# Attention scores in a language-model tower: padded keys against one 32-row matmul per head

## The reference, cut to what matters

```python
q = _bitlinear(x, w_q).reshape(B, T, N_HEADS, D_HEAD)
k = _bitlinear(x, w_k).reshape(B, T, N_HEADS, D_HEAD)
v = _bitlinear(x, w_v).reshape(B, T, N_HEADS, D_HEAD)
attn = jnp.einsum('bqhd,bkhd->bhqk', q, k) * D_HEAD ** (-0.5)
attn = jax.nn.softmax(attn, axis=-1)
out = jnp.einsum('bhqk,bkhd->bqhd', attn, v).reshape(B, T, C)
return _bitlinear(out, w_o)
# around it: h = h + attention(layernorm(h)); then h = h + experts(layernorm(h))
```

## Time and profile before

| | us |
|---|---|
| median of 3 runs | 1735.05 |
| lowest and highest | 1734.72, 1736.13 |
| span of the profiled execution | 1725.5 |
| attention in it, first to last work of the stage | about 276 to 762 |
| a step of the attention in the loop | about 14.7 |
| PE busy over the span | 1609.2 (93%) |
| DVE busy | 1195.8 (69%) |
| ACT busy | 957.5 (55%) |
| POOL busy | 632.1 (37%) |

### The profile page before, as it was taken

One profiled execution on the slowest core, in us unless ns is written; L12 is line 12 of the kernel. 1 busy time (PEld: TensorE's weight loads), 2 busy tenths in 40 slices (PEclk: granted clock), 3 DMA queues, 4 the chain that ended last, 5 costly groups with the idle time before them and its releaser, 6 DMA issues.

```text
span 1725.5 us, 33624 instructions
## 1 busy us (share of the span) xinstructions
PE 1609.2 (93%) x10884; PEld 1354.1 (78%) x10884; DVE 1195.8 (69%) x2292; ACT 957.5 (55%) x1936; POOL 632.1 (37%) x614
## 2 busy tenths in 40 slices
PE   1798886999999999969999999999999999999997
PEld 0444444777777777749999999999999999999996
DVE  2687886999999999866343566666666666655665
ACT  4976774777777777753222355555555555522221
POOL 4655533544444444421750122222222222023343
PEclk9999999999999999989999999999999999999999
DMA  9999981000000000013111366677766777534365
GB/s 311 315 340 341 337 276 53 26 38 37 36 36 36 36 36 31 37 68 115 37 38 49 121 218 232 234 243 251 251 232 234 238 247 247 207 127 139 109 206 196
DMA packets 89868, 274.42 MB, mean 159 GB/s; under 512 B 12640, under 2 KB 13152, under 8 KB 89696
## 3 DMA queue, kind: packets, MB, share of 16 engines
q1 hardware_dynamic: 70688, 223.71, 37.5%
q0 software_dynamic: 17024, 45.97, 8.8%
q10 hardware_dynamic: 2112, 4.19, 0.8%
HBM read 228.14 MB, written 45.69 MB: 159 GB/s over the span
## 4 chain that ended last, share of the span: by engine, by line
PE 54%; DMA 1%; DVE 0%; POOL 0%; ACT 0%; issue 0%; POOLq 0%; DVEq 0%
PE up_ps L1372 12%; PE up_ps L1370 12%; PE up_ps L1371 12%; PE down_ps L1370 6%; PE down_ps L1371 6%; PE down_ps L1372 6%; PE xT_ps L1414 2%; DMA comb<-slot_rows,slot_i 0%; DVE H L1320 0%; DMA xr<-x_turned 0%; DVE xT_lo L1237 0%; POOL comb L1172 0%; ACT xT_hi L1187 0%; DVE H L1312 0%; PE route_ps L1366 0%
## 5 line engine op out<-in xcount | busy, mean ns | idle before, releaser
L1370 PE MATMUL up_ps<-xT_hi,w_hi 128*128 128x256 f32 (+1 forms) x1704 | 483.9, 284 | 8.4 <-DVE xT_lo L1237 8.4
L1372 PE MATMUL up_ps<-xT_hi,w_lo 128*128 128x256 f32 (+1 forms) x1704 | 481.1, 282 | 0.0
L1371 PE MATMUL up_ps<-xT_lo,w_hi 128*128 128x256 f32 (+1 forms) x1704 | 479.1, 281 | 0.0
L1370 PEld LDWEIGHTS up_ps<-xT_hi,w_hi 128*128 128x128 f32 (+1 forms) x1704 | 308.1, 181 | 10.0 <-DVE xT_lo L1237 8.5
L1371 PEld LDWEIGHTS up_ps<-xT_lo,w_hi 128*128 128x128 f32 (+1 forms) x1704 | 308.1, 181 | 1.2
L1372 PEld LDWEIGHTS up_ps<-xT_hi,w_lo 128*128 128x128 f32 (+1 forms) x1704 | 308.1, 181 | 0.0
L1242 DVE TENSOR_TENSOR w_lo<-w_stage,w_hi 128x1408 fp32r<-128x1408 f32 (+1 forms) x123 | 201.4, 1664 | 124.4 <-ACT w_hi L1192 124.2
L1164 POOL DMA_INDIRECT xr<-x_rows,slot_tokens x78 | 120.5, 1544 | 441.6 <-PE xT_ps L1414 362.2
L1219 ACT ACTIVATE h_hi<-h 128x256 fp32r<-128x256 f32 (+1 forms) x213 | 89.0, 418 | 239.3 <-DVE h L1335 239.3
L279 DVE TENSOR_TENSOR W<-W,norm_ps 128x1000 f32<-128x1000 f32 x128 | 147.1, 1190 | 53.5 <-PE norm_ps L354 53.3
L1215 ACT ACTIVATE act_g<-up_ps 128x256 f32<-128x256 f32 (+1 forms) x213 | 79.6, 374 | 182.8 <-PE up_ps L1372 181.4
(11 more groups left out here) (192 smaller groups left out, 2978.0 us busy)
## 6 DMA issues: line engine op xcount, KB each, us to landing
W<-table_t SPq DMA_DIRECT2D x32, 2000.0 KB, 17.2
w_stage<-packed SPq DMA_DIRECT2D x80, 704.0 KB, 6.5
w_stage<-packed SPq DMA_DIRECT2D x40, 768.0 KB, 5.2
slot_rows<-y_rows SPq DMA_DIRECT2D x39, 512.0 KB, 6.7
xr<-x_turned SPq DMA_DIRECT2D x32, 512.0 KB, 3.7
x_rows<-x SPq DMA_DIRECT2D x32, 256.0 KB, 2.0
x_turned<-x2T SPq DMA_DIRECT2D x32, 256.0 KB, 2.0
out<-H SPq DMA_DIRECT2D x32, 256.0 KB, 3.7
```

The source lines that it names most:

```text
L1370: pe.matmul(out, a_hi, b_hi, start=first, stop=False)
L1371: pe.matmul(out, a_hi, b_lo, start=False, stop=False)
L1372: return pe.matmul(out, a_lo, b_hi, start=False, stop=last)
```

## The change

The padded keys `KTx` go, and with them their zeroing, the three copies of POOL, the copy of ACT and three semaphores. `K_T` becomes a pair of buffers and is itself the operand of the scores. Each head has one matmul of its own: 32 rows (its strip j of `QT` and of `K_T`), 128 columns. There are sixteen, four of strip 0, then four of strip 1, and so on; strip j writes bank j of `S`, and the semaphore for a bank is raised by its fourth matmul. So that the head numbers in a bank stay as they were, the columns of the weights for q and k are put in another order on the host (`by_row_tile`): tile m of `QT` now holds on strip j head 4j + m, where it held head 4m + j.

```diff
-        K_T = sb("K_T", [P, KT, T])
-
-        KTx = pair("KTx", [P, KT, GROUPS, T])
+        K_T = pair("K_T", [P, KT, T])
...
-                if proj.yes:
-                    pool.wait_ge(K_scaled, proj.next)
...
-                    after(pool, scores_done, (proj.i - 1) * GROUPS)
-                    for n, j in enumerate(POOL_SLOTS):
-                        at = slice(DH * j, DH * (j + 1))
-                        pool.tensor_tensor(KTx[proj.b][at, :, j, :], K_T[at, :, :], ones[at, :].unsqueeze(1).to_broadcast([DH, KT, T]),
-                                           ALU.mult).then_inc(KTx_by_pool, 1)
-                        pool.wait_ge(KTx_by_pool, proj.i * len(POOL_SLOTS) + n + 1)
...
-            def zero_KTx(b):
-                act.activation(KTx[b][:, :, :, :].rearrange("p m j t -> p (m j t)"), carried_b[:, :].to_broadcast([P, KT * GROUPS * T]),
-                               ACT.Copy).then_inc(KTx_zeroed, 1)
...
-                    after(act, scores_done, (proj.i - 1) * GROUPS)
-                    for j in ACT_SLOTS:
-                        at = slice(DH * j, DH * (j + 1))
-                        act.activation(KTx[proj.b][at, :, j, :], K_T[at, :, :], ACT.Copy).then_inc(KTx_by_act, 1)
...
-                    after(dve, KTx_by_act, proj.i * len(ACT_SLOTS))
-                    after(dve, KTx_by_pool, proj.i * len(POOL_SLOTS))
                     dve.wait_ge(k_done, proj.next)
-                    dve.tensor_tensor(K_T[:, :, :], bank[2][:, :].rearrange("p (k t) -> p k t", k=KT), bc, ALU.mult).then_inc(K_scaled, 1)
+                    dve.tensor_tensor(K_T[proj.b][:, :, :], bank[2][:, :].rearrange("p (k t) -> p k t", k=KT), bc, ALU.mult).then_inc(K_scaled, 1)
...
                     pe.wait_ge(QT_done, score.next)
-                    pe.wait_ge(KTx_by_act, score.next * len(ACT_SLOTS))
-                    pe.wait_ge(KTx_by_pool, score.next * len(POOL_SLOTS))
+                    pe.wait_ge(K_scaled, score.next)
 
                     after(pe, attn_done, score.i)
                     for j in range(GROUPS):
-                        pe.matmul(S[:, j, :], QT[score.b][:, j, :], KTx[score.b][:, j, :, :].rearrange("p j t -> p (j t)"),
-                                  start=True, stop=True).then_inc(scores_done, 1)
+                        at = slice(DH * j, DH * (j + 1))
+                        for m in range(KT):
+                            mm = pe.matmul(S[:, j, m * T:(m + 1) * T], QT[score.b][at, m, :], K_T[score.b][at, m, :], start=True, stop=True)
+                        mm.then_inc(scores_done, 1)
...
+    def by_row_tile(w_t):
+        return np.ascontiguousarray(w_t.reshape(D, GROUPS, PER_GROUP, DH).transpose(0, 2, 1, 3).reshape(D, D))
...
-        "w_q_t": turned(L0_attn_w_q), "w_k_t": turned(L0_attn_w_k), "w_v_t": turned(L0_attn_w_v), "w_o_t": turned(L0_attn_w_o),
+        "w_q_t": by_row_tile(turned(L0_attn_w_q)), "w_k_t": by_row_tile(turned(L0_attn_w_k)), "w_v_t": turned(L0_attn_w_v), "w_o_t": turned(L0_attn_w_o),
```

More of the change, by code:

```diff
@@ L481, in attend @@
         w_in, const_made, dve_const = sem("wr_in"), sem("const_made"), sem("dve_const")
-        KTx_zeroed = sem("KTx_zeroed")
         names = ("rows_scaled stats_done moments_done eps_added rstd_done y_done absmax_done dequant_done quant_done v_scaled z_done xq_done"
-                 " diag_done xq_turned xqT_done spread_done scale_bc_done q_done QT_done k_done K_scaled KTx_by_act KTx_by_pool v_done V_done"
+                 " diag_done xq_turned xqT_done spread_done scale_bc_done q_done QT_done k_done K_scaled v_done V_done"
                  " scores_done max_done exp_done prob_turned probT_done heads_done"
@@ L492, in attend @@
         (rows_scaled, stats_done, moments_done, eps_added, rstd_done, y_done, absmax_done, dequant_done, quant_done, v_scaled, z_done, xq_done,
-         diag_done, xq_turned, xqT_done, spread_done, scale_bc_done, q_done, QT_done, k_done, K_scaled, KTx_by_act, KTx_by_pool, v_done, V_done,
+         diag_done, xq_turned, xqT_done, spread_done, scale_bc_done, q_done, QT_done, k_done, K_scaled, v_done, V_done,
          scores_done, max_done, exp_done, prob_turned, probT_done, heads_done,
@@ L509, in attend @@
         PROBS_BANK = (1, 0, 1, 2)
-        ACT_SLOTS, POOL_SLOTS = (2,), (0, 1, 3)
         def steps(eng, body):
@@ L564, in body @@
                     pool.wait_ge(diag_done, fit.next)
-                if proj.yes:
-                    pool.wait_ge(K_scaled, proj.next)
-                    if isinstance(proj.i, int) and proj.i < 2:
-                        pool.wait_ge(KTx_zeroed, proj.i + 1)
-                    after(pool, scores_done, (proj.i - 1) * GROUPS)
-                    for n, j in enumerate(POOL_SLOTS):
-                        at = slice(DH * j, DH * (j + 1))
-                        pool.tensor_tensor(KTx[proj.b][at, :, j, :], K_T[at, :, :], ones[at, :].unsqueeze(1).to_broadcast([DH, KT, T]),
-                                           ALU.mult).then_inc(KTx_by_pool, 1)
-                        pool.wait_ge(KTx_by_pool, proj.i * len(POOL_SLOTS) + n + 1)
                 if norm.yes:
@@ L674, in body @@
                     act.activation(scale_bc[:, :], bank[3][:, 0:T], ACT.Copy).then_inc(scale_bc_done, 1)
[L675 to L680, removed]
             steps(act, body)
```

## The result

| us | before | changed |
|---|---|---|
| median | 1734.88 | 1796.77 |
| lowest to highest of four | 1732.93 to 1736.13 | 1769.18 to 1843.63 |
| span of the profiled execution | 1725.5 | 1767.2 |
| mean granted clock over the span | 0.991 | 0.959 |

The four executions of the changed kernel took 1769.18, 1773.65, 1819.88 and 1843.63 us, with mean granted clocks of 0.959, 0.958, 0.928 and 0.917. The ratio, taken from the two quicker ones alone, is 1.0219 [1.0195, 1.0242]: slower by 2.2%, where 1730.4 was forecast and 1742 was the end of the range. All four lie above all four of the kernel before. The trace is that of the 1769.18 us execution.

The account below looks back on a forecast made before the run. A ring through DVE, ACT and PE was taken to set the loop's step. Gains of 2.0 (ACT's copy), 1.1 (head start), 1.0 (opening) and 0.5 (end) made 4.6 us, 1735.05 to 1730.4; range 1726 to 1742.

Parts of the forecast that it names:

- 0.54 us of slack: Attention loop: PE waits 0.34 and 0.20 us a step, so scores changing by -0.39 or +0.43 us don't move the step.
- The rival with the fallen clock: Attention: strips side by side leave PE idle 2.4 us before `aq`, clock falls every second step; +22 us, 1757; chance 0.05.
- 1728 for strips side by side: Scores on all four strips at once take 1.1 us; -7.1 us in total; chance 0.12, with the clock falling 0.05.
- The scores, -0.39 us forecast: PE's score matmuls: 0.06 for streaming and loads, 0.20 for row mode, -0.65 for strip overlap; bounds +0.43 and -2.3.
- 0.2 for the mode: Start of the scores on PE: one change to 32-row matmuls costs 0.2 us, between 0.145 and 0.29.
- ACT's copy, 0.07 a step: Loop: without the copy exponentials follow the first maximum directly; 0.07 us a step, 2.0 us over some 28 steps.
- The opening's head start, 1.1 us: Attention's opening: without POOL's copies DVE no longer idles 3.26 us, first scores come earlier; 1.1 us once, bounds 0.5 and 1.8.
- The 1.0 and 0.5 us of the later opening steps and of the end: Shorter scores gain 0.2 us in each of five opening steps, 1.0 us, and 0.5 us around the last sequence.
- The 9.5 us added to the span: Whole kernel: median taken as 9.5 us above the profiled span, turning a span of 1720.9 into 1730.4 us.
- Loads not hidden: Scores: every weight load waits for the matmul ahead on its strip; +3.3 us over 31 steps, 1836 us; chance 0.04.
- full mode changes: Scores: two full row-mode changes and no strip overlap, +0.70 us a step, PE becomes the bound; 1742 us; chance 0.12.
- serial strips: Scores: strips don't overlap, mode changes are cheap, +0.26 us; 1734.0 us in total; chance 0.23.

Follow-up runs that it names:

- e9: Changed kernel with its sixteen score matmuls on 128 rows instead of 32, mixing four heads; 1795.25 us, 0.9925 of the kernel before.
- e4: Changed kernel with four 128-row score matmuls of 398 columns, mixing heads, last 114 columns per bank left out; 1797.19 us, 0.9934 of the kernel before.
- e10: Changed kernel with two unused 64-row matmuls of 512 columns before PE's wait for `aq`; 1760.91 us in one execution, against 1736.10 before.
- e1: Changed kernel with two unused 128-row matmuls of 512 columns before PE's wait for `aq`, in steps with projections; 1806.43 us, 0.9991 of the kernel before.
- e5: Changed kernel with its sixteen 32-row score matmuls reordered, one of each strip in turn; 1955.83 us, 1.0816 of the kernel before.
- e7: Kernel before with only ACT's copy into `KTx` moved to the end of the step; 1731.05 us, 0.9989 of the kernel before.
- e3: Changed kernel with four 128-row score matmuls of 512 columns read from `K_T` without zeros, mixing heads; 1792.84 us, 0.9919 of the kernel before.
- e8: Changed kernel with unused 128-row matmuls in every step with scores: two before the `aq` wait, four where there is no `aq`; 1798.36 us, 0.9947 of before.
- e2: Changed kernel with two unused 32-row matmuls of 512 columns before PE's wait for `aq`; 1832.16 us, 1.0136 of the kernel before.

## Why the prediction was wrong

**The step that failed** is the one that bounded the scores' effect: "In the loop PE has 0.54 us of slack, so neither this nor +0.43 moves the ring". The slack was read at a granted clock of 1.00, and the whole sum was made at the durations of that clock. The change took away what kept the clock there. At the 1.2 GHz level there is no slack: PE is busy for 13.38 of 13.60 us. In the sum the clock stands at nothing, without a reason. The runs showed in its place a granted clock of 0.90 in the loop, which then took 26.2 us more, and that the rows of the matmuls matter for it (e9, e4, e10 beside e1). The text named a granted clock off 1.00 as a sign of error, but gave such a case 0.05, and only together with 2.4 us of waiting in a step. Its step of 14.70 was also only one of a pair of 14.59 and 14.70; the mean was 14.65 before, so the 0.07 should have led to 14.58, not 14.63.

**The rival with the fallen clock** had the right kind of mechanism, at the wrong place and price. It was tied to side-by-side strips; the wait that came was 0.56 us, and at full rows a wait as long did no harm (e4). Its price was +22 us: a loss of 1.5 us in every second step. (Put on its own 1728 for strips side by side, that makes 1750 and not the 1757 written.) The 1.4 us of a short fall is near that 1.5, which was assumed and not worked out, so this is luck; what it lacked were the falls of 13.7 us at 6.0 each, and those of the opening and the end. Where the strips do run side by side (e5), 1757 would have been far too low.

**The scores, -0.39 us forecast.** In the changed kernel's undisturbed steps the records of one strip start 0.111 us apart, with their loads hidden, as forecast. The first pair starts 0.09 late and takes 0.10 more, 0.2 for the mode, as forecast. Strips start 0.554 us apart, five records: three of eight records run beside the next strip's, where two were taken. From the first start to the end of the streaming it is 2.66 us; with the 0.09 ahead of it, 0.68 less than 3.43. The term had the right sign, and the borders were undersized. It is worth nothing, as PE waits 0.56 us for `aq` instead.

**ACT's copy, 0.07 a step:** right; e7 measured it alone. Without any copies the step is 14.50 to 14.52 in e1, e3, e4, e8 and e9, so the rest of what was dropped, POOL's copies and the waits for them, was by difference worth another 0.07, where the main line of the sum said nothing and the bound of 4 us allowed for it. DVE's writing of `aq` takes 0.41 us and of `xq` 0.39, against up to 0.70 at the median of the earlier trace rows. The timelines of DVE and ACT in the changed kernel:

```profile
516.89 1.28 DVE L663 TENSOR_REDUCE neg_max<-S 128x4 f32<-128x512 f32 x2
518.08 0.41 DVE L703 TENSOR_SCALAR aq<-z 128x512 bf16<-128x512 f32 x1
...
520.60 0.39 DVE L719 TENSOR_SCALAR xq<-z 128x512 bf16<-128x512 f32 x1
...
517.60 2.17 ACT L586 ACTIVATE prob<-S,neg_max 128x128 f32<-128x128 f32 x8 [0.58 <-DVE neg_max L663]
```

The first maximum ends at 517.57 (516.89 + 0.68 of one) and the exponentials start 0.03 later, as the prediction said they would; it is the sum that held no clock.

**The opening's head start, 1.1 us:** the mechanism was right and the size too small. DVE's wait of 3.26 is 0.57, and the first maximum comes 20.3 us after the attention's first work instead of 22.7.

```profile
292.64 1.59 DVE L733 TENSOR_SCALAR y<-H,moments,rstd 128x512 f32<-128x512 f32 x1 [0.57 <-POOL rstd L564]
...
297.03 2.48 DVE L663 TENSOR_REDUCE neg_max<-S 128x4 f32<-128x512 f32 x4 [0.43 <-PE S L821]
```

That is 2.4 gained, part of it because the fall at 292.8 did not come. Five microseconds later a fall of 10.2 took it back. The 1.0 and 0.5 us of the later opening steps and of the end are swamped by falls in the changed kernel. e8, with the same scores, has no fall in its opening or before its last scores: the four steps from the second scores to the sixth take 55.90 us there against 56.85 before, 0.24 each where 0.2 was taken, and the last two steps 25.6 against 26.6, 1.0 where 0.5 was taken. How much of this is the scores' and how much the dropped copies' isn't parted.

**From span to median.** The 9.5 us added to the span were not all a fixed cost: in every later run the device time is 2.0 us above the span. The other 7.5 say that the profiled execution of before was a quick one, which would have taken some 1727.5; later executions of that kernel on such a chip took from 1727.84 to 1741.38. This shifts the forecast by nothing, as both sides were treated alike, but of the 41.7 us between the two spans some 7 are that, and the times differ by 34.3 (1769.18 less 1734.88).

**The other rivals.** Loads not hidden, full mode changes, serial strips: none came true. The two that came out slower looked for the loss in the scores, and the scores became faster.

**What stays open.** Which of the falls last 3.4 and which 13.7 us, what mix of few-row matmuls, waits and short turns brings one on, and why the same kernel took 1769 us once and 1844 another time (the slower ones left no trace here; the second trace of the changed kernel shows more falls of the same kind, a clock of 0.85). That rows matter is shown, with one execution of e10 against the mix of short matmuls and a lull. By which measure they do isn't.

## What to carry to other kernels

Slack that an engine has at one clock is no slack at the other: before you take work from TensorE, ask what the clock will do, and look at the granted clock ahead of any busy time afterwards. Matmuls on 32 or 64 rows did not hold the clock here where the same on 128 rows did, so zero-padding that seems wasteful can be what pays for speed; if it is dropped, two spare 128-row matmuls in a wait that costs nothing anyway (e8) gave the clock back in the loop and 0.5% of the time against the kernel before. When a fill is meant to sit behind narrow matmuls, check in the trace that it isn't beside them.

## What the runs showed of the hardware

- **Rows and the clock.** With the same count of matmuls and columns the granted clock of the loop was 0.90 and 0.85 at 32 rows and 1.00 at 128 (e9). With an equal fill of 64 and of 128 rows it was 0.90 and 1.00 (e10, e1). Waits of 0.63 and 0.77 us in alternate steps did no harm at 128 rows (e4).
- **Strips.** Matmuls on another strip can start before all those ahead of them in the code have started: three of eight score records run beside the next strip's at each border, and a fill began at 514.23, ahead of score records that start at 514.33 and later (e2). On four strips in turn, 32 records took 1.17 us where eight of 512 columns took 3.60, a factor of 3.1. The Trainium skill, TensorE: Matmul & The Clock Gate, Part 3 (Measured speedup vs the span model), has 3.07 for four row tiles of 512 columns, and this trace agrees, with 128 columns a matmul; the kernel became 8.2% slower by it all the same.
- **Loads on one strip.** Float32 loads are hidden on the strip that is computing: 0.111 us from start to start in the changed kernel, where streaming alone is 0.107. The Trainium skill, TensorE: Matmul & The Clock Gate, Part 3 (The mechanism), has a load overlap running matmuls only when its row group differs; these starts don't agree, as the earlier trace rows already didn't.
- **How long a fall lasts.** From 485.90 to 499.50 PE was busy for 98% of the time, and the clock stayed at the 1.2 GHz level all the same; other falls with the same work behind them were over in 3.4 us.
